# An attention and mixture-of-experts layer on one core: some early transfers issued by ScalarE's queue, and the steps in a new order

## The chip, the core and the metric

The kernel runs on one core of a Trainium2 chip. The core has five engines, each with its own instruction stream: TensorE (PE; PEld is its weight load), VectorE (DVE), ScalarE (ACT), GpSimd (POOL) and SyncE (SP). Here SP only issues DMA transfers. An engine runs its instructions strictly in order, so an instruction that waits on a semaphore holds up all that is behind it. The metric is the device time of one execution in microseconds.

## The reference

For each of 16 batches of 256 tokens with 128 features:

```
x = x + layernorm(attention(layernorm(x)))     # 16 heads of width 8, softmax(q k / sqrt(128)) v, then w_out
x = x + layernorm(moe(layernorm(x)))           # router to the top 2 of 8 experts (width 64), silu(gate) * up,
                                               # plus one shared expert of width 128
```

Inputs, outputs and weights are float32.

## The kernel before

A batch is one unit of work. Its steps are these, with the engine in brackets.

- `load_x` (SP), `stats1`, `aggr1` (DVE), `rstd1` (POOL) and `apply1` (ACT) are the first layer norm (LN1). `xT` (PE) and `xT_copy` (ACT) transpose the result. `qk` (PE) projects it to queries and keys in the PSUM bank `bank_a`.
- `part1` (ACT), `rest1` (DVE), `part2` (ACT), `part3` (POOL) split queries and keys into three bfloat16 parts, `parts`, whose products together give float32 accuracy.
- `spill` (SP) writes the parts to DRAM (`qk_dram`) in 6 transfers, 3 of queries and 3 of keys. `stack` (SP) reads them back in 4 transfers, 2 into `qs` (queries) and 2 into `ks` (keys), so that the parts of a head lie under each other on 48 partitions. Batch 0 does without DRAM: selection matrices (`lay0a`, `lay0b` on DVE, `lay1`, `lay2` on ACT) are written into `hidden`, and the matmuls `sel1`, `sel2`, `sel3`, `selq` place its parts; the semaphore `laid` counts them, and `kh_copy`, `kl_copy`, `ql_copy`, `qh_copy` move them to `ks` and `qs`.
- `s1_0` to `s1_7` (PE) compute scores of two heads each into one of two PSUM tiles `sc`. `max_0` to `max_7` (DVE, 1.2 us each) take the row maxima. `msplit` (POOL) splits the maxima into three parts, `maxT` (PE) transposes them, `max_copy` (ACT) moves them to `mT`, and `max_stack` (SP, 2 transfers `qs<-mT`) puts them below the queries as three more rows.
- `s2_0` to `s2_7` (PE) compute the scores again, transposed and with the maxima taken off, into the same two tiles `sc`. `exp_0` to `exp_7` (ACT, 1.0 us each) exponentiate. `pv_0` to `pv_3` (PE) multiply with the values.
- The sums go through DRAM once more (`pv_spill`, `den_load`, `pv_load`), are normalised, projected, normed (LN2), added. The expert part follows: LN3, `router`, five times `gu` (PE), `tanh` (ACT), `ha` and `hb` (DVE); expert weights through DRAM (`w_spill`, `w_load`); `hw` (POOL), `down` (PE), LN4, `store`.

Batches overlap. The order of every step on its engine is a table, `TIMES`: for each step a list of 16 ticks, one for each batch. Each engine walks over all ticks, and at each it emits the steps of its own that are due (`due(tick, name)`). The table sets only the order in each engine's stream; when a step really starts is decided by semaphores. `FILL` names places where PE multiplies `ident` by itself into `bank_d`, to stay busy.

All transfers are issued on SP's queue in the order of the table, and PE's scores go by strict turns: `s1` and `s2` of different batches alternate on the two `sc` tiles. The first instructions of `s1(b, 0)` wait for the four stacked transfers of batch b, and those of `s2(b, 0)` wait for the two of the maxima.

Of the kernel before, what the change touches and what calls it, by code (L numbers as in the profile page):

```python
# [12 lines left out]
P = 128  # L13
# [48 lines left out]
    "v_copy": [45, 88, 115, 121, 183, 263, 377, 444, 605, 705, 794, 928, 1033, 1142, 1271, 1395],  # L62
    "pickm": [47],
    "minusm": [50],
    "sel3": [51],
    "load_wd": [53],
    "ql_copy": [55],
    "kh_copy": [56],
    "selq": [59],
    "kl_copy": [60],  # L70
# [110 lines left out]
    "hwl0": [1892],  # L181
    "hwl1": [1894],
    "hwl2": [1895],
    "hwl3": [1896],
}


# [1050 lines left out]
```

## Time and profile before

| | us |
|---|---|
| median of 3 runs | 377.91 (376.65 to 379.62) |
| the profiled execution, device time | 378.36 |
| its span (first to last instruction) | 376.6 |
| busy, PE | 347.9 (92%) |
| busy, DVE | 312.3 (83%) |
| busy, ACT | 268.8 (71%) |
| busy, POOL | 200.2 (53%) |
| DMA engines, mean share on q1 | 48.6% |

Busy time of PE is modelled to the end of each pipelined matmul, so a busy PE is not a PE at its peak. The granted clock of PE is full for 98% of the span. In 40 slices of 9.4 us the page shows the busy tenths of each engine:

```profile
PE   6986898899999999999998999999999999998892
DVE  8498498978989999998997979989998996767661
ACT  5643668788887886877888887787669868964522
```

### The profile page before, as it was taken

What the parts mean: (1) busy time and instruction counts of PE and PEld (TensorE: products, weight loads), DVE (VectorE), ACT (ScalarE), POOL (GpSimd) and SP (SyncE); (2) the same over time, 40 slices, a digit from 0 to 9 for tenths busy, and PEclk for the clock granted to TensorE, in tenths of its full rate; (3) what the DMA queues carried; (4) which work ended last, traced back from release to release, by engine and by line L of the source; (5) the groups of instructions that cost most, each with busy time, mean ns of one, the idle gap of its engine ahead of it and who ended that gap; (6) DMA issues with size and microseconds to landing.
All of it is one profiled execution on the core that took longest, in us unless ns stands there. A gap on an engine that the chain in (4) does not pass through costs nothing.

```text
span 376.6 us, 9905 instructions
## 1 busy us (share of the span) xinstructions
PE 347.9 (92%) x3230; PEld 220.5 (59%) x3230; DVE 312.3 (83%) x788; ACT 268.8 (71%) x511; POOL 200.2 (53%) x518
## 2 busy tenths in 40 slices
PE   6986898899999999999998999999999999998892
PEld 6854444455465657574756565665665556666672
DVE  8498498978989999998997979989998996767661
ACT  5643668788887886877888887787669868964522
POOL 5623134305372584466666455765355648867644
PEclk9899899999999999999999999999999999999998
DMA  2457946716468466367265574734664241222210
GB/s 83 120 136 159 199 98 160 167 39 151 131 157 184 119 167 156 99 145 184 52 190 119 148 168 128 172 100 132 146 150 107 61 127 58 78 71 73 58 30 29
DMA packets 59921, 45.64 MB, mean 121 GB/s; under 512 B 8966, under 2 KB 56966, under 8 KB 59870
## 3 DMA queue, kind: packets, MB, share of 16 engines
q1 hardware_dynamic: 59870, 45.00, 48.6%
q8 instruction: 26, 0.43, 0.5%
q14 instruction: 25, 0.20, 0.2%
HBM read 26.69 MB, written 17.81 MB: 118 GB/s over the span
## 4 chain that ended last, share of the span: by engine, by line
PE 46%; POOL 15%; issue 13%; DVE 9%; ACT 6%; DMA 6%; SPq 4%; POOLq 1%; DVEq 0%; ACTq 0%
PE pvp L648 9%; PE bank_d L818 7%; PE sc L632 6%; PE bank_d L802 6%; PE sc L617 4%; DVE mx L997 4%; PE bank_d L803 4%; POOL hidden L1206 4%; POOL rstd L1139 3%; PE bank_a L701 3%; DMA qs<-mT 2%; ACT pr L846 2%; PE bank_d L775 1%; SPq L534 1%; DMA rwb<-rw_dram 1%
## 5 line engine op out<-in xcount | busy, mean ns | idle before, releaser
L997 DVE TENSOR_REDUCE mx<-sc 128x4 f32<-128x1024 f32 x128 | 154.0, 1218 | 20.1 <-PE sc L617 18.7
L846 ACT ACTIVATE pr<-sc 128x1024 f32<-128x1024 f32 x128 | 130.5, 1024 | 25.5 <-PE sc L632 24.2
L648 PE MATMUL pvp<-pr,va 128*32 128x256 f32 x1024 | 68.4, 385 | 0.0
L802 PE MATMUL bank_d<-x3T,wg_sb 128*128 128x256 f32 x160 | 54.8, 424 | 3.2 <-DVE hidden L1095 2.8
L632 PE MATMUL sc<-qs,ks 51*128 51x256 bf16 x512 | 50.2, 277 | 6.6 <-DMA qs<-mT 4.3
L617 PE MATMUL sc<-ks,qs 48*128 48x256 bf16 x512 | 49.4, 274 | 3.1 <-DMA ks<-qk_dram 1.0
L1206 POOL TENSOR_TENSOR hidden<-hidden,rwb 128x256 f32<-128x256 f32 x60 | 42.8, 728 | 16.4 <-DMA rwb<-rw_dram 16.4
L803 PE MATMUL bank_d<-x3T,wu_sb 128*128 128x256 f32 x160 | 47.7, 380 | 0.0
L1139 POOL TENSOR_TENSOR rstd<-vareps,mhalf 128x2 f32<-128x2 f32 x64 | 44.5, 695 | 0.0
L929 ACT ACTIVATE th<-bank_d 128x256 f32<-128x256 f32 x80 | 30.4, 382 | 16.7 <-PE bank_d L803 15.7
L648 PEld LDWEIGHTS pvp<-pr,va 128*32 128x32 f32 x1024 | 26.7, 109 | 25.4 <-issue 13.1
L818 PE MATMUL bank_d<-wd_sb,hidden 128*128 128x128 f32 x320 | 39.5, 279 | 1.9 <-POOL hidden L1206 1.7
L1089 DVE SCALAR_TENSOR_TENSOR ha<-th,bank_d 128x256 f32<-128x256 f32 x80 | 32.4, 407 | 9.4 <-ACT th L929 9.0
L1134 POOL TENSOR_TENSOR vareps<-mv,eps 128x2 f32<-128x2 f32 x64 | 12.4, 195 | 52.0 <-DVE mv L980 49.7
L818 PEld LDWEIGHTS bank_d<-wd_sb,hidden 128*128 128x128 f32 x320 | 37.1, 192 | 4.8 <-issue 2.3
L632 PEld LDWEIGHTS sc<-qs,ks 51*128 51x128 bf16 x512 | 16.4, 95 | 37.2 <-issue 15.2
L802 PEld LDWEIGHTS bank_d<-x3T,wg_sb 128*128 128x128 f32 x160 | 24.3, 189 | 19.1 <-issue 18.5
L617 PEld LDWEIGHTS sc<-ks,qs 48*128 48x128 bf16 x512 | 18.1, 95 | 26.7 <-issue 8.8
L1095 DVE SCALAR_TENSOR_TENSOR hidden<-ha,bank_d 128x256 f32<-128x256 f32 x80 | 32.6, 411 | 1.1 <-PE bank_d L818 0.2
L803 PEld LDWEIGHTS bank_d<-x3T,wu_sb 128*128 128x128 f32 x160 | 30.7, 192 | 4.3
L1150 POOL TENSOR_TENSOR parts<-rest,parts 128x512 bf16<-128x512 f32 x16 | 18.5, 1155 | 23.7 <-ACT parts L874 23.7
L1029 DVE RECIPROCAL rden<-den 128x256 f32<-128x256 f32 x14 | 24.4, 1741 | 0.2
(113 smaller groups left out, 488.6 us busy)
## 6 DMA issues: line engine op xcount, KB each, us to landing
rwb<-rw_dram SPq DMA_DIRECT2D x30, 256.0 KB, 4.3
qk_dram<-parts SPq DMA_DIRECT2D x30, 192.0 KB, 2.6
qs<-qk_dram SPq DMA_DIRECT2D x30, 192.0 KB, 4.6
ks<-qk_dram SPq DMA_DIRECT2D x30, 192.0 KB, 4.9
qk_dram<-parts SPq DMA_DIRECT2D x30, 128.0 KB, 2.6
pv_dram<-pv_sb SPq DMA_DIRECT2D x14, 256.0 KB, 2.3
x_sb<-in_L_attn_x_dram SPq DMA_DIRECT2D x16, 128.0 KB, 2.7
out_dram<-x SPq DMA_DIRECT2D x16, 128.0 KB, 1.9
```

Of the source, the lines that this page charges most:

```text
L617: mm = pe.matmul(sc[pair][:, u, c, :], q[rows, s, c * P:(c + 1) * P], k[rows, s, :], start=True, stop=True)
L632: mm = pe.matmul(sc[pair][:, u, c, :], k[rows, s, c * P:(c + 1) * P], q[rows, s, :], start=True, stop=True)
L648: mm = pe.matmul(pvp[32 * j:32 * j + 32, g, :], values[:, X * c + 4 * g + j, 32 * tt:32 * tt + 32], pr[:, k, c * N:(c + 1) * N], start=(tt ...
L802: pe.matmul(bank_d[bank][:, 0:N], wg_sb[:, ORDER[n], :], x3T[b % 2][:], start=True, stop=True)
L803: pe.matmul(bank_d[bank][:, N:2 * N], wu_sb[:, ORDER[n], :], x3T[b % 2][:], start=True, stop=True).then_inc(gu_done, 1)
L818: mm = pe.matmul(bank_d[0][:, c * P:(c + 1) * P], src, wd_sb[:, n, :], start=(n == 4), stop=(n == 3))
L846: nc.scalar.activation(pr[:, 2 * s:2 * s + 2, :].rearrange("p k n -> p (k n)"), sc[PAIR["s2", b, s]][:].rearrange("p u c n -> p (u c n)"), ...
L997: nc.vector.tensor_reduce(mx[b % 2][:, :, :, s].rearrange("p c u -> p u c"), sc[PAIR["s1", b, s]][:], AX.X, ALU.max).then_inc(max_done, 1)
L1089: nc.vector.scalar_tensor_tensor(out=ha[n][:], in0=th[n][:], scalar=1.0, in1=bank_d[BANK[n]][:, 0:N], op0=ALU.add, op1=ALU.mult).then_inc( ...
L1095: nc.vector.scalar_tensor_tensor(out=hb[b % 2][:, ORDER[n], :], in0=ha[n][:], scalar=0.5, in1=bank_d[BANK[n]][:, N:2 * N], op0=ALU.mult, o ...
L1139: nc.gpsimd.tensor_tensor(rstd[L][p][:], vareps[L][p][:], mhalf[:], ALU.pow).then_inc(rstd_done[L], 1)
L1206: nc.gpsimd.tensor_tensor(hw[b % 2][:, n, :].rearrange("p (t g r) -> p t g r", t=TT, g=4), hb[b % 2][:, n, :].rearrange("p (t g r) -> p t ...
```

## The change

The functions that issue one transfer of a spill, a stack or the maxima are taken out of SP's loop and given the issuing engine as an argument. For batch 1 the three key transfers of the spill (`spillA`) and the two key transfers of the stack (`stackA`) are issued by ACT, those of the queries by SP as before. For batch 0 the two transfers of the maxima are issued by ACT, right behind `max_copy`. For all other batches SP issues everything, as before. The table `TIMES` is a new one throughout. `FILL` loses most entries; a new table `FILL_SCORES` puts such matmuls in front of some `s1` and `s2`, behind the wait for the free tile and ahead of the wait for the transfers. Of LN1's neighbours at the start, `lay0a` now stands behind `aggr1` of batch 0, and `lay2` behind `xT_copy` of batch 0.

```diff
 FILL = {
-    "maxT": {0: 9},
+    "maxT": {0: 1},
     "qk": {0: 1},
-    "s1_3": {0: 2},
-    "s1_4": {0: 2, 1: 1},
-    "s1_5": {0: 2, 2: 1},
-    "s2_0": {0: 2},
-    "s2_4": {0: 2, 1: 1},
-    "s2_5": {0: 1},
     "sel1": {0: 2},
-    "xT": {0: 12, 3: 1},
+    "xT": {0: 17, 4: 1},
+}
+FILL_SCORES = {
+    ("s1", 0, 3): 1,
...
+    ("s1", 3, 7): 1,
...
+    ("s2", 1, 3): 2,
 }
...
+        def spill_k(engine, b, n):
+            first, slots = SLOTS_K[n]
+            dst = qk_dram[b % 2][1, first:first + slots].rearrange("a d u x n -> (d u x) a n")
+            engine.dma_start(dst, parts[b % 2][:, 1, 0:slots, :]).then_inc(qk_spilled[b % 2], DMA)
...
-                        sp.dma_start(dst, parts[b % 2][:, 1, 0:slots, :]).then_inc(qk_spilled[b % 2], DMA)
+                        spill_q(sp, b, n)
+                        if b > 1:
+                            spill_k(sp, b, n)
...
+                        stack_q(sp, b, u)
+                        if b > 1:
+                            stack_k(sp, b, u)
-                if (b := due(tick, "max_stack")) is not None:
+                if (b := due(tick, "max_stack")) is not None and b:
...
+                pair = PAIR["s1", b, s]
+                turn(sc_empty[pair])
+                fill_scores("s1", b, s, pair)
                 if b and s == 0:
                     pe.wait_ge(qk_stacked[b % 2], landed1(4, b))
...
             for tick in TICKS:
+                if due(tick, "spillA") is not None:
+                    act.wait_ge(part3_done, 2)
+                    for n in range(3):
+                        spill_k(act, 1, n)
+                if due(tick, "stackA") is not None:
+                    act.wait_ge(qk_spilled[1], landed1(6, 1))
+                    for u in range(2):
+                        stack_k(act, 1, u)
+                if due(tick, "max_stack") == 0:
+                    act.wait_ge(max_copied, 1)
+                    for u in range(2):
+                        stack_max(act, 0, u)
```

The first place that matters is SP's queue from the spill of batch 1 on. `qk_dram1<-parts1` is that spill, `qs1<-qk_dram1` and `ks<-qk_dram1` are the stack of batch 1, `qk_dram0<-parts0` is the spill of batch 2, `qs0<-mT0` are the maxima of batch 0. Before:

```order
L534 DMA qk_dram1<-parts1 128x3x256
L537 DMA qk_dram1<-parts1 128x3x256
...
L544 DMA qs1<-qk_dram1 48x2048
L546 DMA ks<-qk_dram1 48x2048
...
L534 DMA qk_dram0<-parts0 128x3x256
...
L478 DMA ks<-minus 3x4x2048 x2
L551 DMA qs0<-mT0 3x8x256 x2
L469 DMA x_sb6<-in_L0_attn_x_dram 128x2x128
L544 DMA qs2<-qk_dram0 48x2048
```

Now, on the same queue:

```order
L478 DMA qk_dram1<-parts1 128x3x256
L478 DMA qk_dram1<-parts1 128x2x256
L478 DMA qk_dram1<-parts1 128x256
L486 DMA qs1<-qk_dram1 48x2048 x2
L502 DMA x_sb5<-in_L0_attn_x_dram 128x2x128
L511 DMA ks<-minus 3x4x2048 x2
L478 DMA qk_dram0<-parts0 128x3x256
...
L483 DMA qk_dram1<-parts1 128x256
L486 DMA qs2<-qk_dram0 48x2048
```

The keys of batch 1 and the maxima of batch 0 have left the queue, the `minus` rows have moved ahead of the spill of batch 2, and the spill of batch 3 (the last `qk_dram1<-parts1`) has moved ahead of the stack of batch 2.

The second place is ACT's stream over the same stretch. `parts1<-rest1` is `part2` of batch 1, `va1` and `va2` are `v_copy` of batches 1 and 2, `mT0` is `max_copy` of batch 0, and `xn` is `apply1`. Before:

```order
L877 CAST ks<-sc0 112x1024
L874 CAST parts1<-rest1 128x2x256
L863 COPY xT0<-bank_a 128x256
L884 CAST qs0<-pvp 112x512
L885 CAST qs0<-bank_d0 112x512
L871 CAST parts0<-bank_a 128x2x256
L831 ACTIVATE xn1<-x_sb3,shift1_1,rstd1_1 128x128 x2
L874 CAST parts0<-rest0 128x2x256
L892 COPY va1<-bank_a 128x32x8
```

Now, from `part2` of batch 1 (`xn1<-x_sb3` stands just ahead of it):

```order
L919 CAST parts1<-rest1 128x2x256
L908 COPY xT0<-bank_a 128x256
L929 CAST qs0<-pvp 112x512
L930 CAST qs0<-bank_d0 112x512
L937 COPY va1<-bank_a 128x32x8
L483 DMA qk_dram1<-parts1 128x3x256
L483 DMA qk_dram1<-parts1 128x2x256
L483 DMA qk_dram1<-parts1 128x256
L916 CAST parts0<-bank_a 128x2x256
L490 DMA ks<-qk_dram1 48x2048 x2
L937 COPY va2<-bank_a 128x32x8
L919 CAST parts0<-rest0 128x2x256
```

Seven transfers now stand in ACT's stream (the two `qs0<-mT0` come right behind `max_copy`), and `apply1` of batch 3 has moved ahead of `part2` of batch 1.

The third place is DVE's start. `hidden<-ident_bf` are the copies of `lay0a` and `lay0b`, `st1_0<-x_sb0` is `stats1` of batch 0. Before:

```order
L953 MEMSET hidden 128x896
L988 COPY hidden<-ident_bf 128x8x24 x2
L988 COPY hidden<-ident_bf 128x8x2x8 x2
L988 COPY hidden<-ident_bf 128x8x8 x2
L991 MEMSET rw0 128x16
L991 MEMSET rw1 128x16
L973 BN_STATS st1_0<-x_sb0 128x6 x2
```

Now:

```order
L998 MEMSET hidden 128x896
L1033 COPY hidden<-ident_bf 128x8x2x8
L1033 COPY hidden<-ident_bf 128x8x8 x2
L1018 BN_STATS st1_0<-x_sb0 128x6 x2
L1025 BN_AGGR mv1_0<-st1_0 128x2 x2
L1033 COPY hidden<-ident_bf 128x8x24 x2
```

Three of the six copies and two memsets have moved from ahead of the first layer norm to behind it.

## Rows read from the trace of the kernel before

**Rows 1.** Busy us by stretch: PE, PEld, DVE, ACT, POOL; clock, DMA share, GB/s

```profile
20.00:47.00 27.00, 21.84 (x166) 12.83 (x166) 20.49 (x28) 12.56 (x24) 6.30 (x15) 0.94 0.76 172
...
80.00:320.00 240.00, 232.96 (x2311) 143.03 (x2304) 217.15 (x535) 191.12 (x354) 135.53 (x351) 1.00 0.53 132
```

**Rows 2.** The chain that ended last, 19 to 39 us: start, us, what

```profile
19.57 1.17 POOL parts L1150
...
23.32 2.40 DMA qk_dram<-parts
...
33.79 4.27 DMA qs<-mT
```

**Rows 3.** Timeline of SP's queue: start, us of issuing, line, transfer

```profile
20.75 0.37 SPq L534 DMA_DIRECT2D qk_dram<-parts  x1
...
27.04 0.42 SPq L546 DMA_DIRECT2D ks<-qk_dram  x1
...
32.69 2.97 SPq L551 DMA_DIRECT2D qs<-mT  x2
...
54.28 1.50 SPq L551 DMA_DIRECT2D qs<-mT  x2
```

**Rows 4.** Timeline of PE: start, us, instruction, idle before it and its releaser

```profile
7.59 0.44 PE L691 MATMUL bank_a<-ident,xn 128*128 128x128 f32 x2 [1.29 <-ACT xn L831]
...
8.58 1.81 PE L701 MATMUL bank_a<-xT,wqk_sb 128*128 128x256 f32 x4 [0.33 <-ACT xT L863]
...
16.30 1.03 PE L701 MATMUL bank_a<-xT,wqk_sb 128*128 128x256 f32 x4
...
28.64 2.27 PE L655 MATMUL bank_d<-ident 128*128 128x128 f32 x18
...
32.59 0.39 PE L617 MATMUL sc<-ks,qs 48*128 48x256 bf16 x4 [1.05 <-DMA ks<-qk_dram]
...
38.10 0.39 PE L632 MATMUL sc<-qs,ks 51*128 51x256 bf16 x4 [1.63 <-DMA qs<-mT]
...
57.29 0.39 PE L632 MATMUL sc<-qs,ks 51*128 51x256 bf16 x4 [0.97 <-DMA qs<-mT]
```

**Rows 5.** Timeline of DVE, columns as in rows 4

```profile
4.29 0.27 DVE L973 BATCH_NORM_STATS2 st<-x_sb 128x6 f32<-128x128 f32 x1
...
19.73 4.62 DVE L997 TENSOR_REDUCE mx<-sc 128x4 f32<-128x1024 f32 x4 [0.94 <-PE sc L617]
...
33.03 4.62 DVE L997 TENSOR_REDUCE mx<-sc 128x4 f32<-128x1024 f32 x4 [1.12 <-PE sc L617]
39.45 1.23 DVE L997 TENSOR_REDUCE mx<-sc 128x4 f32<-128x1024 f32 x1 [1.80 <-PE sc L617]
43.19 1.23 DVE L997 TENSOR_REDUCE mx<-sc 128x4 f32<-128x1024 f32 x1 [2.50 <-PE sc L617]
...
47.76 0.68 DVE L1020 TENSOR_TENSOR rest<-bank_a,parts 128x512 f32<-128x512 f32 x1
```

**Rows 6.** The copies of `lay0a` and `lay0b` by source line: ns min/median/max

```profile
L988 DVE COPY hidden<-ident_bf x6: 206/261/1498, 2.0 to 4.1; 128x192 bf16<-128x192 bf16 x2, 128x128 bf16<-128x128 bf16 x2, 128x64 bf16<-128x64 bf16 x2
```

**Rows 7.** Busy time in five shorter stretches, columns as in rows 1

```profile
8.80:12.20 3.40, 3.40 (x13) 2.89 (x13) 2.42 (x16) 1.77 (x4) 1.29 (x5) 0.50 0.40 94
21.00:25.70 4.70, 4.12 (x34) 2.69 (x34) 4.70 (x5) 1.98 (x4) 0.03 (x1) 1.00 0.70 197
26.00:32.60 6.60, 4.64 (x36) 3.33 (x36) 5.42 (x13) 1.51 (x4) 2.86 (x9) 1.00 0.94 185
39.50:42.90 3.40, 3.28 (x16) 1.74 (x16) 1.18 (x1) 1.94 (x5) 1.03 (x1) 0.51 1.06 160
73.70:77.10 3.40, 3.40 (x15) 1.95 (x14) 2.19 (x3) 1.61 (x2) 0.91 (x4) 0.50 0.50 152
```

**Rows 8.** Timeline of ACT: `apply1` of one batch, and `max_copy` of batch 0

```profile
21.53 0.88 ACT L831 ACTIVATE xn<-x_sb,shift,rstd 128x128 f32<-128x128 f32 x2
...
31.59 0.37 ACT L853 CAST mT<-bank_a 48x256 bf16<-48x256 f32 x1 [2.57 <-PE bank_a L670]
```

**Rows 9.** Waits of PE over the whole span: us in total, times, longest

```profile
PE sc L632 <- DMA qs<-mT: 4.3, 4, 1.6
```

More of the change, by code:

```diff
@@ L55 @@
-    "load_wgu": [33],
[6 rows of a table removed]
[L62 to L70, printed above, removed]
-    "s1_0": [64, 107, 165, 229, 283, 391, 493, 607, 700, 831, 932, 1069, 1179, 1290, 1386, 1515],
-    "qh_copy": [67],
-    "s1_1": [68, 114, 173, 238, 307, 407, 522, 621, 723, 852, 952, 1085, 1196, 1309, 1403, 1530],
@@ L179 @@
[L179 to L184 removed]
+    "load_x": [0, 12, 13, 15, 38, 95, 142, 185, 206, 208, 218, 280, 401, 473, 551, 822],
+    "lay0b": [14],
+    "stats1": [16, 23, 24, 50, 51, 139, 161, 221, 237, 247, 353, 378, 478, 664, 1013, 1106],
+    "lay1": [18],
+    "load_wout": [19],
+    "aggr1": [20, 27, 34, 52, 62, 160, 181, 231, 250, 347, 461, 526, 608, 683, 1119, 1169],
@@ new lines @@
+    "wv": [35],
+    "part1": [37, 61, 88, 110, 151, 209, 297, 432, 534, 666, 759, 876, 1008, 1118, 1230, 1354],
+    "rest1": [40, 66, 89, 112, 153, 217, 305, 441, 553, 670, 764, 882, 1010, 1124, 1235, 1359],
+    "sel1": [41],
+    "load_wgu": [42],
[5 rows of a table added]
+    "v_copy": [49, 80, 96, 129, 191, 262, 354, 459, 593, 711, 787, 931, 1055, 1177, 1265, 1432],
+    "sel3": [55],
+    "minusm": [57],
+    "ql_copy": [59],
+    "kh_copy": [60],
+    "selq": [63],
+    "pickm": [64],
+    "kl_copy": [65],
[3 rows of a table added]
+    "qh_copy": [76],
@@ new lines @@
+    "max_1": [78, 120, 178, 243, 314, 420, 533, 629, 725, 859, 967, 1084, 1203, 1318, 1430, 1550],
+    "s1_2": [79, 123, 180, 248, 324, 422, 535, 630, 734, 862, 980, 1096, 1210, 1326, 1440, 1553],
+    "spill": [None, 81, 108, 124, 188, 289, 341, 474, 587, 717, 803, 911, 1024, 1151, 1252, 1386],
+    "spillA": [82],
[5 rows of a table added]
+    "stack": [None, 91, 134, 146, 212, 327, 425, 524, 607, 752, 857, 989, 1086, 1193, 1288, 1419],
+    "stackA": [92],
+    "max_4": [93, 135, 195, 265, 343, 447, 559, 655, 775, 891, 1007, 1132, 1237, 1345, 1458, 1586],
@@ L599, in turn, with fill_scores @@
                     pe.wait_ge(*empty)
+            def fill_scores(kind, b, s, pair):
+                for _ in range(FILL_SCORES.get((kind, b, s), 0)):
+                    pe.matmul(sc[pair][:, 0, 0, 0:P], ident[:], ident[:], start=True, stop=True)
             def s1(b, s):
+                pair = PAIR["s1", b, s]
+                turn(sc_empty[pair])
+                fill_scores("s1", b, s, pair)
                 if b and s == 0:
@@ L621, in s2 @@
             def s2(b, s):
+                pair = PAIR["s2", b, s]
+                turn(sc_empty[pair])
+                fill_scores("s2", b, s, pair)
                 if s == 0:
```

141 lines of the change are left out of this document (71 added, 70 removed), and 156 rows, old and new, of the table TIMES.

## The prediction

> **What bounds the kernel now.** I read the busy time by stretch first [rows 1]. From 80 to 320 us PE is busy for 232.96 of 240 us and DVE for 217.15, so 97% and 90%. There two engines share the bound, and each loses time only by waiting for the other. The start is different: from 20 to 47 us PE is busy for 21.84 and DVE for 20.49 of 27. What is to be had is there, since the new table leaves the tail with the same steps in nearly the same sequence.
>
> The chain of waits says what the start waits for [rows 2]. It passes from POOL's `part3` of batch 1 into SP, stays in SP's queue and its transfers from 20.75 to 38.06 us, and ends with the 4.27 us of the maxima transfer. SP's timeline [rows 3] shows why. The spill of batch 1 is issued from 20.75 on, the last of its six at 23.32. The four of the stack follow, the last at 27.04. Behind them stand the spill of batch 2 and the `minus` rows, so the maxima, which ACT had copied by 31.96 [rows 8], are issued only at 32.69, and these two issues take 2.97 us where the next pair takes 1.50.
>
> PE and DVE show the price [rows 4, 5]. PE gets batch 1's scores going at 32.59, released by the keys of the stack, and batch 0's `s2_0` at 38.10, released by the maxima. DVE waits 1.12 us ahead of the first maximum of batch 1, 1.80 ahead of the fifth, 2.50 ahead of the sixth. The last ends at 47.8.
>
> PE's granted clock is the other loss. It is at half, 1.2 GHz, for 3.4 us from 8.8, from 39.5 and from 73.7 us [rows 7]. The first time comes after PE sat idle for 1.29 us ahead of `xT`, and `qk` then takes 1.81 us where the next takes 1.03 [rows 4]; the second comes after the waits for the maxima.
>
> **The change part by part.** Times are against the profiled span of 376.6 us.
>
> *Start of LN1.* `stats1` of batch 0 begins at 4.29, behind six copies. Now three copies stand ahead of it. The first of the six took 1498 ns, the shortest 206, the median 261 [rows 6]. The long one comes first in time, beside POOL's memset of `hidden`, and in the new order the first is still beside it. So the three take about 1.50 + 0.21 + 0.21 = 1.9 us from 1.96, and `stats1` starts at about 3.9: 0.4 us gained. The bound if the long copy were gone would be 1.7.
> The Trainium skill, "SBUF — State Buffer", on the shared port pair, says that a GpSimd instruction and a VectorE instruction in a two-port mode lock each other out for the whole instruction. By that rule it is the first copy, whichever it is, that waits, and the gain is the 0.4 us; the one row of 1498 ns agrees.
>
> *Fills ahead of `xT`.* Seventeen instead of twelve. Five more are ten records, at 2.27 us for 18 [rows 4] about 1.2 us, which covers the 1.29 us in which PE sat idle. If the clock then stays up, `qk` takes 1.03 instead of 1.81, and the first selection matmuls, which also lie ahead of 12.2 us, save some 0.5 more (an estimate: one us of them at half clock). I take 0.9 of these 1.3, because the clock may fall all the same. If it does, the fills cost nothing but the stretch at half clock stays. With the 0.4 above, `laid` and the copies behind it are 1.3 us earlier.
>
> *`apply1` of batch 3 ahead of `part2` of batch 1.* It adds 0.88 us of ACT to the chain, as the two `apply1` activations take [rows 8]. `part3` of batch 1, which ended at 20.73, now ends at 20.3: 0.4 us gained, not 1.3.
>
> *Spill of batch 1 on two queues.* Six issues at about 0.5 us become three beside three. No transfer was issued by ACT in this trace; the nearest rows are SP's, from 0.33 us for a quiet one to 1.5 (half of 2.97) for one behind a full queue [rows 3], and I take SP's 0.5, since ACT's own queue is empty. Issuing then ends at 21.8. The DMA engines bound the rest: from 21.0 to 25.7 they were busy for 0.70 of 4.7 us [rows 7], that is 3.3 us, so the last lands no sooner than about 20.3 + 0.6 + 3.3 = 24.2, with 0.6 as my estimate for the first packets to set out. Before it landed at 25.72: 1.5 us gained, of which 0.4 were there already.
> The Trainium skill, "DMA: Bandwidth & Descriptors", section "Issuing engines are not separate DMA queues", speaks against expecting more: all queues run on the same 16 DMA engines, and issuing from several saves only the sequencer's time. By it this step is worth at most 1.5 us of saved issuing; the row of 3.3 us busy limits it to 1.1, so here it is the row that is tighter.
>
> *Stack of batch 1.* Two issues beside two: the last is issued at 24.7 instead of 27.04. It landed at 32.5, 5.5 us later, in a stretch in which the DMA engines were busy for 0.94 of 6.6 us [rows 7], because SP put the spill of batch 2 right behind it. Now `x` of batch 5, `minus` and the wait for `part3` stand between, so I take 4.7 us for it. It lands at 29.4, and the first maximum of batch 1 starts at 29.9 instead of 33.03: 3.1 us gained. If the landing stays 5.5 us, it is 2.3.
>
> *Maxima of batch 0 on ACT.* `maxT` follows `s1_1` of batch 1, so the copy can start about 1.2 us after 29.5 and, with its 0.37 [rows 8], ends at 31.1. Two issues take 1.5 to 2.1 us and the landing 1.5 to 2.3 behind them (the pair at 54.28 ended at 55.78 and released PE at 57.29 [rows 3, 4]). `s2_0` starts at 34.1 to 35.5, I take 34.8: 3.3 us earlier than 38.10.
>
> *DVE after that.* With four maxima from 29.9 it waits about 1.1 us for the fifth instead of 1.80. Ahead of the sixth PE has `s2_1`, `qk`, `s2_2`, `s1_5`. At full clock this wait is 1.4 instead of 2.50; at half clock it stays. So batch 1's last maximum is earlier by 3.1 + 0.7 + 1.1 = 4.9 at full clock, by 3.8 at half. I take the middle, 4.4.
>
> *What ACT's transfers cost.* ACT is busy for 12.56 of these 27 us [rows 1]. But ACT stands still at the wait for `qk_spilled`, until 24.2. Behind it `v_copy` of batch 2 holds `bank_a`, which `xT` of batch 3 needs, and `s1_7` of batch 0 stands behind that on PE. By my times `v_copy` ends at 25.5. DVE's first maximum moves from 19.73 to 18.4 [rows 5], and seven at 1.16 with one `rest1` at 0.6 bring it to 27.1, when it wants `s1_7`. So it costs nothing up to 1 us of delay, and one for one beyond.
>
> *The other fills.* 39 before, 38 now. One in front of an `s1` takes 0.2 us behind the wait for the tile while DVE works 1.2 us on the other: hidden. They are meant for the clock; the stretch from 73.7 may go, which is worth about 1 us. I take half: 0.5.
>
> *The rest of the table.* From 80 us on the counts of instructions are the same. PE waits four times for the maxima, 4.3 us in all [rows 9], two of them in the start above. I take zero for the new sequence, with 3 us to either side as the bound: that is about what one more or fewer wait in each fourth batch makes.
>
> The sum is 4.4 + 0.5 = 4.9 us. Span 376.6 - 4.9 = 371.7. The profiled execution took 378.36, so 1.8 lie around the span, and it was 0.45 above the median of the runs. That gives 371.7 + 1.8 - 0.45 = 373.0; I predict **373.2 us**. All figures are of one execution, and about 1% is what a measurement of this kernel can tell from no change, here 3.8 us.
>
> **The rivals.**
> *A: as forecast, 0.55.* The gain at 47 us is kept, because both bounding engines are near their limit from there and simply start earlier. 370 to 374.1.
> *B: gained and given back, 0.20.* SP now has the spill of batch 3 ahead of the stack of batch 2, and in some batches (2 and 6) about 3 us of PE's work stand between the maxima transfer and `s2_0`, where there were 4 and 9. Two waits of 1.0 to 1.6 us, as [rows 4, 9] show, leave 4.9 - 2.6 = 2.3: about 375.8.
> *C: little gained at the start, 0.12.* The transfers share the DMA engines, which were busy for 0.94 from 26 to 32.6 us, and the clock falls in all three places. Then the start gives 0.4 + 1.1 at the spill and some of the maxima, 1.5 to 2 us: about 376.2. The chain [rows 2], which is in SP's issuing and not only in landing, speaks against it.
> *D: slower, 0.13.* The mechanism is the maxima reaching PE late in the middle. A wait of 1.6 us there was followed by 3.4 us at half clock, in which PE loses up to 1.7 more: 3.3 a time. The gain of 4.9 is used up after one and a half of them, and from three on (9.9) the kernel is slower by more than 1%: about 383. For it speaks that PE goes by strict turns; against it that the clock was full from 80 to 320 us in spite of two such waits.
>
> **How the numbers follow.** Faster by over 1% (below 374.1) is A: 0.55. Within 1% are B and C: 0.32. Slower is D: 0.13. The range is 370.0 to 378.0: below lies the case that the middle also gains 3, above it the bulk of D.
>
> **What would show it.** In the profile after: `stats1` at 3.9; `qk` of batch 0 near 1.0 us; the stack's release of `s1_0` of batch 1 near 29.4; `s2_0` of batch 0 near 34.8 and DVE's last maximum of batch 1 ending at 43.4; the half clocks from 8.8 and 39.5 gone. The sum is wrong if ACT's issues take over 1 us each, if PE is held at `xT` of batch 3, or if the stretch from 47 to 320 us is not as long as before.

## The result, and the profile after

The changed kernel is slower: 385.71 us median of 4 runs (382.79 to 389.03), where the kernel before had 377.28 on the same chip. The ratio is 1.0207, with an interval of 1.0143 to 1.0271; it leaves out the run of 389.03, which counts as a slow one. So the kernel is slower, clear of noise; whether by more than 2% is open. The forecast was 373.2, so the sign was wrong too.

| | before | after |
|---|---|---|
| profiled execution, us | 378.36 | 389.03 |
| its span, us | 376.6 | 387.2 |
| granted clock over the span | 0.983 | 0.965 |
| TensorE at half clock, us: mean over the runs | 11.3 (105 runs) | 22.9 (4 runs) |

The last line is worked out from each run's span and mean granted clock, as 2 x (1 - clock) x span. By this a mean clock of 0.983 is 12.8 us at half clock, 3.4% of the span; the 98% given for the kernel before is the mean clock, not the share of the time at full clock. The profiled execution of after is the longest of its four, so its later stretches at half clock are more than the median run has. Its waits up to 41 us are not peculiar to it: e3, the same program up to there, shows them within 0.2 us.

Up to 28 us the times are near the forecast ones or earlier. PE's and DVE's timelines of the changed kernel, columns as in [rows 4]:

```profile
1.51 5.59 PE L688 MATMUL bank_d<-ident 128*128 128x128 f32 x34 [1.51 <-POOL ident L1167]
...
8.07 1.10 PE L734 MATMUL bank_a<-xT,wqk_sb 128*128 128x256 f32 x4 [0.33 <-ACT xT L908]
...
27.42 0.61 PE L630 MATMUL sc<-ident 128*128 128x128 f32 x4
31.17 0.61 PE L649 MATMUL sc<-ks,qs 48*128 48x256 bf16 x8 [3.14 <-DMA ks<-qk_dram]
...
36.09 1.20 PE L744 MATMUL bank_a<-wv_sb,xT 128*128 128x128 f32 x4 [1.36 <-ACT xT L908]
38.86 0.61 PE L665 MATMUL sc<-qs,ks 51*128 51x256 bf16 x4 [1.58 <-issue]
```

```profile
1.95 1.62 DVE L1033 COPY hidden<-ident_bf 128x128 bf16<-128x128 bf16 x3
3.49 0.48 DVE L1018 BATCH_NORM_STATS2 st<-x_sb 128x6 f32<-128x128 f32 x2
...
17.76 4.62 DVE L1042 TENSOR_REDUCE mx<-sc 128x4 f32<-128x1024 f32 x4 [0.73 <-PE sc L649]
...
31.60 2.36 DVE L1042 TENSOR_REDUCE mx<-sc 128x4 f32<-128x1024 f32 x2 [2.67 <-PE sc L649]
...
40.78 1.23 DVE L1042 TENSOR_REDUCE mx<-sc 128x4 f32<-128x1024 f32 x1 [4.08 <-PE sc L649]
```

DVE's first maximum starts at 17.76 instead of 19.73 [rows 5], 2.0 us earlier. But 1.2 of these lie in the one execution of the kernel before that was profiled. e4, e5 and e10, described below, run the old program up to there; in their traces the clock stays full at 8.8 us. PE and DVE of e10:

```profile
7.59 0.44 PE L691 MATMUL bank_a<-ident,xn 128*128 128x128 f32 x2 [1.06 <-ACT xn L831]
...
8.58 1.10 PE L701 MATMUL bank_a<-xT,wqk_sb 128*128 128x256 f32 x4 [0.33 <-ACT xT L863]
```

```profile
18.48 4.62 DVE L997 TENSOR_REDUCE mx<-sc 128x4 f32<-128x1024 f32 x4 [0.94 <-PE sc L617]
```

Against these three (18.48 to 18.50) the changed kernel gains 0.7 us, and at batch 1's scores nothing: they come at 31.17, where the profiled before has 32.59 but e4 31.33 and e10 30.69. `s2_0` of batch 0 starts at 38.86, behind the 38.10 of before [rows 4]. SP's queue and ACT with its queue show the transfers (for a queue: start, us of issuing):

```profile
19.76 1.78 SPq L478 DMA_DIRECT2D qk_dram<-parts  x3
23.94 0.81 SPq L486 DMA_DIRECT2D qs<-qk_dram  x2
...
27.03 1.59 SPq L478 DMA_DIRECT2D qk_dram<-parts  x1
28.67 1.79 SPq L483 DMA_DIRECT2D qk_dram<-parts  x1
```

```profile
19.77 1.86 ACTq L483 DMA_DIRECT2D qk_dram<-parts  x3
...
23.94 0.84 ACTq L490 DMA_DIRECT2D ks<-qk_dram  x2
...
32.58 0.36 ACT L898 CAST mT<-bank_a 48x256 bf16<-48x256 f32 x1 [3.00 <-PE bank_a L703]
32.98 2.49 ACTq L494 DMA_DIRECT2D qs<-mT  x2
35.57 0.37 ACT L908 COPY xT<-bank_a 128x256 f32<-128x256 f32 x1 [2.62 <-issue]
```

The stack is issued by 24.78, 2.7 us earlier than the 27.46 of [rows 3], yet lands at 31.12: 6.3 us behind. The maxima keep ACT issuing for 2.49 us, and `xT_copy` of batch 4, behind them in ACT's program, starts 2.62 us late. The chain of waits has the same two pieces (start, us, what):

```profile
24.34 6.78 DMA ks<-qk_dram
...
32.98 1.35 ACTq L494
34.33 0.37 issue
34.70 0.76 ACTq L494
...
35.57 0.38 ACT xT L908
```

And the clock, in busy time by stretch, columns as in [rows 1]; the second group is the stretches at half clock:

```profile
20.00:47.00 27.00, 19.72 (x126) 10.95 (x126) 16.33 (x18) 8.73 (x16) 3.21 (x6) 0.75 0.87 189
...
80.00:320.00 240.00, 230.49 (x2266) 142.84 (x2264) 215.53 (x520) 187.66 (x346) 130.54 (x335) 0.99 0.53 135
...
26.00:32.60 6.60, 3.46 (x27) 2.28 (x26) 3.61 (x4) 2.21 (x6) 3.06 (x6) 0.96 1.03 199
```

```profile
32.10:45.70 13.60, 10.66 (x61) 5.37 (x60) 7.06 (x8) 4.18 (x6) 0.00 (x0) 0.50 0.94 201
49.10:55.90 6.80, 6.37 (x50) 2.49 (x52) 2.55 (x6) 2.93 (x4) 3.04 (x9) 0.50 0.00 1
```

Between 20 and 47 us PE is busy for 2.1 us less than before and DVE for 4.2 less. PE sat idle for 3.14 us ahead of the stack, and from 32.1 us it was at half clock for 13.6 us on end. Before, 18 fill products, 2.27 us, stood in front of that wait; the change has 4 there (27.42), and 2 of `maxT`'s behind it. (A fill of the tables shows as two products in a trace: the 9 of `maxT` are these 18.)

### The profile page after: what moved, and what is told of

Read it like the earlier page. It is cut to its first block, busy times and chain, and to the rows that moved or that the text cites. A ratio compares the mean times of both kernels' runs of the same rounds, so it can differ in the third digit from the quotient of the medians.

```text
span 387.2 us, 9900 instructions
## 1 busy us (share of the span) xinstructions
PE 350.5 (91%) x3228; PEld 222.7 (58%) x3228; DVE 311.5 (80%) x788; ACT 267.8 (69%) x511; POOL 201.0 (52%) x518
## 4 chain that ended last, share of the span: by engine, by line
PE 40%; issue 20%; POOL 14%; DVE 9%; DMA 7%; ACT 6%; SPq 2%; ACTq 1%; POOLq 1%; DVEq 0%
PE pvp L681 7%; PE bank_d L851 6%; PE sc L665 6%; PE bank_d L835 5%; POOL hidden L1251 4%; DVE mx L1042 4%; PE sc L649 4%; PE bank_d L836 3%; POOL rstd L1184 3%; DMA qs<-mT 2%; PE bank_a L734 2%; ACT pr L891 2%; DMA ks<-qk_dram 2%; PE bank_d L688 2%; DVE ha L1134 1%
## 5 line engine op out<-in xcount | busy, mean ns | idle before, releaser
L681 PE MATMUL pvp<-pr,va 128*32 128x256 f32 x1024 | 71.0, 396 | 0.0
L649 PE MATMUL sc<-ks,qs 48*128 48x256 bf16 x512 | 50.4, 278 | 5.3 <-DMA ks<-qk_dram 3.1
L1251 POOL TENSOR_TENSOR hidden<-hidden,rwb 128x256 f32<-128x256 f32 x60 | 42.2, 729 | 21.8 <-DMA rwb<-rw_dram 19.8
L851 PE MATMUL bank_d<-wd_sb,hidden 128*128 128x128 f32 x320 | 41.0, 285 | 3.6 <-POOL hidden L1251 3.6
L974 ACT ACTIVATE th<-bank_d 128x256 f32<-128x256 f32 x80 | 30.6, 383 | 17.2 <-PE bank_d L836 15.8
L851 PEld LDWEIGHTS bank_d<-wd_sb,hidden 128*128 128x128 f32 x320 | 38.7, 199 | 6.6 <-issue 6.1
L835 PEld LDWEIGHTS bank_d<-x3T,wg_sb 128*128 128x128 f32 x160 | 24.2, 188 | 19.3 <-issue 19.0
L649 PEld LDWEIGHTS sc<-ks,qs 48*128 48x128 bf16 x512 | 19.0, 96 | 26.1 <-DVE mx L1042 7.9
```

The source lines that it names most:

```text
L649: mm = pe.matmul(sc[pair][:, u, c, :], q[rows, s, c * P:(c + 1) * P], k[rows, s, :], start=True, stop=True)
L681: mm = pe.matmul(pvp[32 * j:32 * j + 32, g, :], values[:, X * c + 4 * g + j, 32 * tt:32 * tt + 32], pr[:, k, c * N:(c + 1) * N], start=(tt ...
L835: pe.matmul(bank_d[bank][:, 0:N], wg_sb[:, ORDER[n], :], x3T[b % 2][:], start=True, stop=True)
L851: mm = pe.matmul(bank_d[0][:, c * P:(c + 1) * P], src, wd_sb[:, n, :], start=(n == 4), stop=(n == 3))
L1251: nc.gpsimd.tensor_tensor(hw[b % 2][:, n, :].rearrange("p (t g r) -> p t g r", t=TT, g=4), hb[b % 2][:, n, :].rearrange("p (t g r) -> p t ...
```

## The experiments

Ratios are to the kernel before on the same chip; a median stands beside the others only roughly, since those of the kernel before went from 376.4 to 378.2 between chips and hours. So versions are compared by their ratios, 0.1% being 0.38 us. One chip each had e1 to e4, e5 to e8, e9 to e12, and e13 to e16.

| run | median us | ratio, interval | half clock, mean us |
|---|---|---|---|
| changed kernel | 385.71 | 1.0207, 1.0143 to 1.0271 | 22.9 |
| e1_all_sp | 383.61 | 1.0136, 1.0059 to 1.0212 | 19.7 |
| e2_fills | 379.43 | 1.0037, 0.9997 to 1.0077 | 7.3 |
| e7_fills_sp | 376.21 | 1.0000, 0.9957 to 1.0042 | 5.0 |
| e13_keys_act | 376.31 | 0.9960, 0.9919 to 1.0001 | 6.7 |
| e14_maxima_act | 382.91 | 1.0141, 1.0082 to 1.0201 | 13.1 |
| e17_keys_act_13_5 | 377.61 | 0.9999, 0.9956 to 1.0041 | 7.2 |
| e5_act_only | 382.66 | 1.0177, 1.0113 to 1.0241 | 21.1 |
| e3_head_new | 395.18 | none | 37.3 |
| e4_head_old | 382.57 | 1.0131, 1.0019 to 1.0243 | 17.2 |
| e12_old_head | 377.91 | 1.0002, 0.9961 to 1.0043 | 8.7 |
| e6_sp_behind | 379.77 | 1.0093, 1.0052 to 1.0134 | 10.5 |
| e9_stack_alone | 383.76 | 1.0145, 1.0026 to 1.0263 | 17.6 |
| e10_maxT_fills | 377.71 | 1.0011, 0.9970 to 1.0051 | 15.3 |
| e8_start | 376.28 | 0.9959, 0.9914 to 1.0004 | 10.2 |
| e16_start_only | 378.24 | 0.9981, 0.9936 to 1.0026 | 12.0 |
| e11_start_fills | 377.38 | 1.0025, 0.9991 to 1.0058 | 5.7 |
| e15_start_six | 376.64 | 0.9975, 0.9945 to 1.0005 | 3.8 |

**All transfers back on SP, and longer fills.** e1 puts the three groups of transfers back on SP in the new order; e2 keeps them on ACT and lengthens two fills; e7 does both.

```diff
     # e1_all_sp, e7_fills_sp (the three blocks on ACT go)
-                        if b > 1:
-                            spill_k(sp, b, n)
+                        spill_k(sp, b, n)
-                if (b := due(tick, "max_stack")) is not None and b:
+                if (b := due(tick, "max_stack")) is not None:
     # e2_fills, e7_fills_sp
-    ("s1", 1, 0): 2,
+    ("s1", 1, 0): 16,
+    ("s2", 0, 0): 8,
```

> The changed kernel with its new table, but all transfers issued by SP again. If the issuing by ACT is what costs (ACT stood at its own two maxima issues for 2.5 us, and the copy behind them was 2.6 us late), this comes back by 2 to 4 us, to about 381. If the new order at the start and PE's half clock in it are what costs, it stays within 2 us of the changed kernel (383 to 388) or is worse, since SP's queue holds the maxima behind two spills again.

> The changed kernel with more ident matmuls ahead of two waits: 16 instead of 2 ahead of the first scores of batch 1, 8 ahead of the first second-pass scores of batch 0. If the loss is PE's half clock from 32 to 46 and from 49 to 56 us after a wait of 3.1 us without work, the clock stays full there and the time falls by 5 to 8 us, to about 378. If the late transfers alone cost, the clock row changes and the time stays within 1.5 us of 385.

> The changed kernel's order with the longer fills (16 and 8), and every transfer issued by SP as before. It undoes ScalarE's issuing at a clock that the fills hold up. Theory 1 (ScalarE's issuing of the maxima costs, the rest of it gains nothing): the first second-stage product of batch 0 starts 1.5 to 2.5 us earlier than the 40.3 with ScalarE's issuing, and the time is 377 to 379, 1 to 2 us under 379.4. Theory 2 (ScalarE's issuing is not what costs; the order is): within 0.7 us of 379.4, or slower by the later stack.

By the ratios, fills alone take 1.7% off, 6.4 us, and 1.4%, 5.1 us, with all transfers on SP (e1 to e7). Moving the transfers to SP takes off 0.7% with the short fills; the intervals overlap, so e1 alone decides nothing. With the long fills it is 0.9%, 3.5 us, between e6 (which is e2 over again, see below) and e7 on the same chip; between e2 and e7, on two chips, it is 0.4%. So there are two causes, the fills' being the larger. In e2 PE does not stand idle ahead of the stack, and the clock holds there; the maxima still hold ACT, and ahead of `s2_0` the clock falls:

```profile
27.79 3.73 PE L631 MATMUL sc<-ident 128*128 128x128 f32 x32
31.46 0.61 PE L650 MATMUL sc<-ks,qs 48*128 48x256 bf16 x8
...
37.01 3.32 PE L631 MATMUL sc<-ident 128*128 128x128 f32 x16
40.26 0.39 PE L666 MATMUL sc<-qs,ks 51*128 51x256 bf16 x4
```

The upper 32 products take 3.73 us at full clock, the lower 16 take 3.32, most of it at half. In e7 those 16 took 2.05 and `s2_0` stood at 37.27, 3.0 us earlier, more than either theory had.

**Which of ACT's transfers.** Both with e2's fills: e13 leaves the keys on ACT and puts the maxima back on SP, e14 the other way round.

```diff
     # e13_keys_act
-                if (b := due(tick, "max_stack")) is not None and b:
+                if (b := due(tick, "max_stack")) is not None:
-                if due(tick, "max_stack") == 0:
-                    act.wait_ge(max_copied, 1)
-                    for u in range(2):
-                        stack_max(act, 0, u)
```

> The changed order with the longer fills (16 and 8); ScalarE's queue issues the keys of batch 1's spill and stack, SP the two maxima transfers of batch 0. With all on SP this was 376.2 us, with keys and maxima on ScalarE 379.4. Theory 1 (the maxima transfers are what costs on ScalarE: they stand there for 2.5 us at a time when its queue holds x's copies and the exponentials): 376 to 377.3. Theory 2 (the keys on ScalarE cost as well, by the 0.4 us that the stack lands later): 377.5 to 379.5.

> The fourth corner beside the three: longer fills, ScalarE issues the maxima transfers alone, SP all keys. Theory 1: 378.5 to 380, ScalarE stands about 2.5 us at the two transfers, and the first second-stage product of batch 0 starts at 39.5 to 40.5. Theory 2 (the maxima are late only where the DMA engines are also loaded by ScalarE's keys): 376 to 378, with the two issues under 1.5 us.

Keys on ACT: 376.31 (theory 1). Maxima on ACT: 382.91, slower than both theories had. The ratios are 1.8% apart on one chip, 6.8 us. ACT's own timeline of e14 first, then SP's queue, ACT and PE of e13:

```profile
33.22 2.10 ACTq L495 DMA_DIRECT2D qs<-mT  x2
35.43 0.37 ACT L899 COPY xT<-bank_a 128x256 f32<-128x256 f32 x1 [2.23 <-issue]
```

```profile
32.84 1.50 SPq L495 DMA_DIRECT2D qs<-mT  x2
...
33.39 0.37 ACT L905 COPY xT<-bank_a 128x256 f32<-128x256 f32 x1 [0.59 <-PE bank_a L725]
...
37.11 0.39 PE L666 MATMUL sc<-qs,ks 51*128 51x256 bf16 x4
```

In e14 `s2_0` starts at 39.67. The path is: two issues hold ACT for 2.1 us, `xT_copy` of batch 4 waits behind them, PE has `v` of batch 3 ahead of `s2_0` in its program and stands until that copy frees the buffer, and its fills, now at half clock, follow. How the 6.8 us divide is not shown. 6.4 us more at half clock would be 2.4 at the 0.38 found below; `s2_0` is 2.6 later, part of it by that clock. Nor is it shown why the maxima alone on ACT measure slower than keys and maxima together: e14's `s2_0` is no later than e2's 40.26, and its ratio is 1.0141 against 1.0037 (e2) and 1.0093 (e6).

**ACT's issuing in the old order.** e5 has before's table and fills, and the three groups on ACT.

> The kernel before with its own order and its own fills; of the change only one part is left: ScalarE's queue issues the key transfers of batch 1's spill and stack and batch 0's two maxima transfers. Theory 1 (the transfers are limited by what the 16 DMA engines carry, not by which queue issues them, and ScalarE stands while it issues): the stack of batch 1 lands where it did, within 0.7 us of 32.5, ScalarE stands 2 to 2.5 us at the maxima transfers (2.49 in the changed kernel), the first second-stage product of batch 0 starts 1 to 2.5 us behind 38.1, and the time is 378.5 to 381.5 us against 377. Theory 2 (the issuing on two queues is what the change gains by, and the order lost it): the stack lands at 29.5 to 31, the second-stage product starts at 36 to 37, and the time is 375 to 376.5.

It is 1.8% slower by itself, on theory 1's side and beyond its bounds: the two maxima issues take 2.70 us, and `s2_0` starts at 40.91. Here the trace has a wait behind the keys as well; what it alone costs was not run. ACT stands at its wait for `qk_spilled` in a place where the old order has `v_copy` behind it, PE then waits for that copy, and again behind the maxima:

```profile
26.98 0.41 PE L717 MATMUL bank_a<-ident,xn 128*128 128x128 f32 x2 [2.23 <-ACT va L930]
...
37.10 0.68 PE L737 MATMUL bank_a<-wv_sb,xT 128*128 128x128 f32 x4 [2.20 <-ACT va L930]
40.91 0.61 PE L658 MATMUL sc<-qs,ks 51*128 51x256 bf16 x4 [1.72 <-DVE mx L1035]
```

**What limits the stack's landing.** e6 moved three SP steps in the table; since SP has nothing else between them, its queue stayed as it was, and the run is e2 over again: 379.77 beside 379.43, with ratios of 1.0093 and 1.0037. So far apart can one kernel lie on two chips. e9 is e7 with a real wait.

```diff
     # e9_stack_alone; fills 10 instead of 16
                 if (b := due(tick, "load_x")) is not None:
+                    if b == 5:
+                        sp.wait_ge(qk_stacked[1], landed1(4, 1))
```

> The changed kernel with the longer fills of the run before (16 and 8 products in place of 2 and 0), and three steps of SP moved: the load of x's tile 5, the minus ones' load and batch 2's spill stand behind the first scores of batch 1 and no longer right behind batch 1's stack. Theory 1 (the stack lands late, 6.4 us behind its last issue, because its packets share the DMA engines with what SP puts right behind it): the stack lands 1.5 to 2.5 us earlier, at 29 to 30 instead of 31.2, and the first max of batch 1 with it; what this gives at the end is open, since batch 2's spill is later by 3 to 5 us, 377 to 380. Theory 2 (the landing is the time that the stack's own descriptors take, whatever is behind them): it lands at 30.9 to 31.5 again, and the kernel is slower than the 379.4 of the kernel it is built from, 380 to 383, by batch 2's later stack.

> The changed order with all transfers on SP and the longer fills (10 products before batch 1's first scores, 8 before batch 0's second stage), and one wait more: SP waits until batch 1's stack has landed before it issues x's tile 5, the minus ones and batch 2's spill. (A run before this one was meant to move these behind by their steps alone, but nothing of it changed SP's own order.) Theory 1 (the stack's landing 5.6 to 6.4 us behind its last issue is partly the traffic put behind it): the stack lands at 29.3 to 30.3 instead of 31.2, and since batch 2's spill then comes 2 to 3 us later and its stack with it, the time is 376 to 378.5 against the 376.2 without the wait. Theory 2 (the 768 KB of the stack alone take this long): it lands at 31.0 to 31.6, and the time is 377.5 to 380.

PE's timeline of e9, then of e1, in which SP goes on issuing behind the stack:

```profile
30.34 0.61 PE L650 MATMUL sc<-ks,qs 48*128 48x256 bf16 x8 [0.42 <-DMA ks<-qk_dram]
```

```profile
30.75 0.61 PE L647 MATMUL sc<-ks,qs 48*128 48x256 bf16 x8 [2.75 <-DMA ks<-qk_dram]
```

With nothing behind it the stack, issued by 25.83, lands 4.5 us later; with `x`, `minus` and the next spill behind it, issued by about 25.7, 5.0 us later. These are single executions. e10, which has the whole spill of batch 2 right behind the stack, lands it 4.5 us behind its last issue too, and the profiled before 5.1. So the traffic behind is not shown to cost anything, and most of the time is the 768 KB themselves. These are the traces in which PE waited for the stack, from the first of its four issues to the landing of the last:

| trace | keys issued by | first issue | landed | us |
|---|---|---|---|---|
| before, e4, e16 | SP | 25.74, 24.49, 24.54 | 32.54, 31.28, 31.04 | 6.8, 6.8, 6.5 |
| e1, e10, e9 | SP | 23.98, 24.45, 24.11 | 30.70, 30.63, 30.29 | 6.7, 6.2, 6.2 |
| after, e3, e17 | ACT | 23.94, 24.19, 24.55 | 31.12, 31.29, 31.97 | 7.2, 7.1, 7.4 |

From two queues the last issue ends 0.9 us earlier (24.78 in after, 25.7 in e1), and the stack takes 0.3 to 1.2 us longer. What the second queue saved in issuing it did not save in landing. In e9 the landing is theory 1's and the time neither's: by the ratios it is 5.5 us slower than e7. Batch 2's spill starts at 32.48 instead of 28.2, the maxima behind it are issued only from 38.00, and PE stands for 4.64 us ahead of `s2_0`.

**The halves of the table.** e3 is the changed kernel up to batch 0's `pv_3` with before's order behind; e4 before's order up to `pv_copy` of batch 0 and the new one behind; e12 is e4 with the change's start and with fills of 4 and 8.

> The new order and ACT's transfers up to pv_3 of batch 0 (about 60 us), and from there the old order. If the whole loss arises in the first 60 us, this is as slow as the changed kernel, 383 to 388. If the new order of the middle costs too (its lag grew by 2 to 4 us between 68 and 387 us), this is 2 to 4 us faster than the changed kernel, about 381.

> The reverse: the old order and SP's transfers up to pv_copy of batch 0, and the new order behind it. If the loss arises in the first 60 us, this is within 1.5 us of the kernel before, 377. If the new order of the middle costs by itself, it is 380 to 381.

> The change's start, before's order from there to the end of batch 0's attention, the change's order from there on; all transfers on SP, fills as in the run that had the start alone (376.3). It tells whether the order behind 47 us is worth anything. Theory 1 (the rest of the table is neutral; the changed kernel loses ahead of it): 375.5 to 377, as the run with the start alone. Theory 2 (the rest of the table loses 1.5 us or more by itself): 378 to 380. Theory 3 (it gains, and the head hides it): under 375.

e3 tells nothing of the change, and no ratio is given for it: at the seam PE waited 6.52 us for a DVE maximum at 62 us, a stall that neither kernel has. e12 is level with before, theory 1: where the fills are long, the order behind batch 0 neither gains nor loses by more than 0.4%. e4 is 1.3% slower, outside both its cases and by an interval that starts at 0.2%; its mean at half clock is 17.2 us against 8.7 in e12. Its trace has 10.2 us at half from 33.1 on, which is inside the part with before's order, where the profiled before has 3.4. So e4 does not tell whether the new order behind, without fills, loses by itself.

**The start, and the fills of the kernel before.** e16 is before with the change's start alone; e8 adds fills of 4 and 8 ahead of the two waits; e11 six more small ones; e15 takes 6 instead of 9 ahead of `maxT`, and 5 and 6 ahead of the two waits. e10 is before with one number changed:

```diff
     # e10_maxT_fills
-    "maxT": {0: 9},
+    "maxT": {0: 1},
```

> The kernel before with the change's start alone (the layout copy behind LayerNorm's first aggregate, 17 fills instead of 12 ahead of x's first transpose), no other fill and no other order. The prediction priced these at 1.3 us of its 4.9, and half clock at 8.8 us would be gone. Theory 1 (the gain arrives at the end): 374.5 to 376, and batch 0's last max 1 to 2 us earlier. Theory 2 (it is swallowed by the wait for batch 1's stack, or by half clock later): 376.5 to 378.

> The kernel before with two things of the change and no more: the new order up to the first projection (the layout copy behind LayerNorm's first aggregate, the 17 fills ahead of x's first transpose), and fills while TensorE waits for batch 1's stack and batch 0's maxima (4 and 8 products). All transfers on SP, before's order behind. Theory 1 (what the change gains ahead of 20 us is real, and the loss comes behind it from the clock and the transfers): no half clock at 8.8 and at 39.5 us, batch 0's last max 0.4 to 1.5 us earlier, and the time is 373.5 to 376. Theory 2 (the start is worth nothing, the stack's landing swallows it, and half clock costs little): 376.5 to 378.

> The kernel before with the change's start (the layout copy behind LayerNorm's first aggregate, 17 fills ahead of x's first transpose) and fills ahead of waiting scores: 4 and 8 products at batch 1's first scores and batch 0's second stage as in the run before, and now 4, 2, 1, 1, 1, 1 more at six places of batches 1 to 3, where TensorE waits in that run's trace. Theory 1 (what is left over 372 is half clock in the first 80 us): the stretches at half clock at 56.0 and 73.1 go, and the time is 373 to 375.5. Theory 2 (the fills only stand in the way of work, or the clock falls elsewhere): 376 to 378.

> A candidate: the kernel before with the change's start, 6 fills ahead of the maxima's transpose instead of 9 (that transpose waited 2.3 us behind them, and the kernel before with 1 of the 9 had its batch 1 end 3.2 us earlier, though at half clock for 6.8 us), and 5, 6, 4, 2, 1, 1, 1, 1 fills at waiting scores of batches 0 to 3. Theory 1 (both gains add where the clock holds): 373 to 375.5. Theory 2 (the time at the end hangs on where the clock falls later, which fills up to 70 us don't set): 376 to 378.

> The kernel before with one number changed: 1 fill instead of 9 (2 products instead of 18, 2.27 us) ahead of the transpose of batch 0's maxima, as the change has it. Theory 1 (these fills carry TensorE's clock over the wait for batch 1's stack, and half of the change's loss is their going): half clock from about 32 us for 7 to 14 us, and a time of 379 to 382 us against 376.5. Theory 2 (the clock falls elsewhere for other causes; the fills are worth their place, no more): 375.5 to 377.5.

None differs from before by more than its interval. Batch 0's last maximum, which ends at 29.98 in the profiled before, ends at 28.25 to 29.40 in e16, e8, e11 and e15. But in e4 and e10, which lack the new start, it ends at 28.76 and 28.74, so what the start is worth lies between 0.7 us lost and 0.5 gained. A reason for the loss is in the traces: the 34 products of the 17 fills take 5.5 to 7.0 us, and in e11 and e16 `xT` starts behind them only at 8.30 and 7.70, where the old start has it at 7.58 to 7.60 in each trace. In e11:

```profile
1.51 6.95 PE L688 MATMUL bank_d<-ident 128*128 128x128 f32 x34 [1.51 <-POOL ident L1155]
8.30 0.38 PE L724 MATMUL bank_a<-ident,xn 128*128 128x128 f32 x2
```

In e10 PE stood for 2.15 us ahead of `maxT` and was at half clock from 29.8 us for 6.8 (with all its fills the old program has 3.4 us in this stage in one trace and 10.2 in another, e4). The mean at half was 15.3 us, against 10.7 for the kernel before on the same chip. By the price below that is 1.7 us; the interval reaches to 1.9. So in the old order these fills are worth little, where in the new one the wait was 3.14 us, the late maxima followed it, and the stretch was 13.6.

**The best of it.** e17 is e13 with 13 and 5 fills.

> The run with the keys on ScalarE, the maxima on SP and long fills (ratio 0.996), with 13 and 5 fills instead of 16 and 8: in that run's trace the fills ended at 31.3 and 37.1 us, right against the products behind them, so that they may hold back what has landed. Theory 1 (the fills hid 0.3 to 0.7 us at each of the two places, and the clock holds): batch 0's second stage starts at 36.3 to 36.8 instead of 37.1, ratio 0.990 to 0.996. Theory 2 (nothing had landed before, or the clock falls again once the fills are shorter): 0.996 to 1.003.

Level with before, theory 2. The stack released PE at 32.01 and the maxima at 37.60, both behind the fills' end. In this execution 16 fills would have ended ahead of 32.01 and hidden nothing, and 8 at about 38.0 (35.99, where they start, and the 2.05 us of e7's), 0.4 us too late. No version beat the kernel before by more than the measurement tells.

**What half clock costs.** Over 105 runs of the kernel before, all one program, the time rises by 0.38 us for each us at half clock (a line through the runs; correlation 0.77; 0.33 to 0.42 chip by chip). Such a line can't tell what the clock costs from what the late data cost that made it fall. But it fits where only fills were added: the changed kernel to e2 has 15.6 us less at half and is 6.4 faster (5.9 by the line), and e1 to e7 14.7 less and 5.1 faster (5.6). By it the 11.6 us more at half clock in the changed kernel are 4.4 of its 7.8 us (2.07%). What the other 3.4 are is not separately shown. The nearest is e6 against e7, 3.5 us for ACT's transfers, but with 5.5 us more at half clock in it, 2.1 by the line: no run has the maxima on ACT at a clock that held.

## Why the prediction was wrong

*Start of LN1: right, and undersized.* Forecast 3.9, measured 3.49, with the three copies at 1.62 us in all. The longest of the copies is now 1466 ns, beside the same memset of `hidden` on POOL, though another form stands in front; that agrees with the rule on the shared port pair on the Trainium skill's page "SBUF — State Buffer", "Who interferes with whom", by which of a VectorE instruction in a two-port mode and a GpSimd instruction the second to start is blocked until the first has ended. No run was made to test it.

*Fills ahead of `xT`: met by luck.* `qk` took 1.10 us and there is no half clock at 8.8. But with the twelve old fills e4, e5 and e10 have the same 1.10 and the same full clock behind idle times of 1.06 to 1.73 us. The forecast took for a property of the kernel what one of four traces of the old start shows, so its 0.9 us are not the fills' doing. Nor are the fills free, as the forecast had them: in e11 and e16 they delay `xT`.

*`apply1` of batch 3 ahead: not shown.* `part3` of batch 1 ended at 19.74 (forecast 20.3), but in e4 and e10, in the old order, at 19.5.

*Spill of batch 1: right in its times.* Issued by 21.6 (forecast 21.8), landed by 23.9 (forecast 24.2). The second queue is not why: e1, with all six on SP, landed at 23.96. The 0.6 us for the first packets came from no row; in the trace of the kernel before, the DMA engines stay idle from the first issue at 20.75 to about 21.65, 0.9 us.

*Stack of batch 1: the first step that failed.* The last issue began at 24.34 (forecast 24.7), but "I take 4.7 us for it" was 6.8, counted like the forecast from that issue's start (6.3 from its end). The reasoning that `x`, `minus` and a wait for `part3` would leave the engines free was wrong: DMA's share from 26 to 32.6 us is 1.03 where it was 0.94 [rows 7]. Nor was batch 2's spill what made it 5.5 before: e10 has that spill behind and took 4.9. The gain is 1.4 us at PE against the profiled before, not 3.1, and none against e4, e10 and e16. The rule "Issuing engines are not separate DMA queues" on the Trainium skill's page "DMA: Bandwidth & Descriptors", by which a second engine saves only the sequencer's time, is borne out, and more strongly than I used it: e7, with the keys on one queue, is level with e13, and the landings from two queues took longer.

*Maxima of batch 0 on ACT: failed by its sign.* Forecast `s2_0` at 34.8; measured 38.86. The copy `mT` was done at 32.94 instead of 31.1, by the late stack; the two issues took 2.49 us, above my bound of 2.1; and `s2_0` started 3.4 us behind them, where the landing was to take up to 2.3 (the profile names no releaser; that it was the landing is by elimination). SP did the two in 1.5 us (e13).

*What ACT's transfers cost: the step behind the wrong sign.* I checked only the wait for the spill, and that part holds: `v_copy` of batch 2 ended at 25.25 (forecast 25.5). I did not list what stands behind the maxima's issues on ACT, which is `xT_copy` of batch 4, and behind that `v` and `s2_0` on PE. For the keys the step holds in the new order (e13 against e7); in the old one e5's trace has a wait of 2.23 us behind them.

*The other fills: failed.* "39 before, 38 now" counted them and did not ask where they stand. I priced them at a gain of 0.5; in the new order they are the largest loss. What the number hid is that the wait for the stack had 18 products in front of it and got 4. Long fills there (32 products) and ahead of `s2_0` (16) recover 5.1 to 6.4 us; that is more than the kernel before had, and in the old order taking 16 of the 18 away cost nothing that can be told (e10).

*DVE after that* falls with its inputs: batch 1's last maximum came 2.1 us later than before, not 4.4 earlier.

*The rest of the table: right at zero where fills hold the clock* (e12); without them it is open (e4). But the head's gain is not at the end even where the clock holds: in e7 batch 1's last maximum is 2.1 us earlier than before, batch 2's 0.2, and the median is level. From there PE waits for ACT's exponentials, 0.73 and 0.90 us, and 0.95 at 58.57; the old order has 0.20 at 39.62 and 0.43 at 58.80:

```profile
43.22 0.71 PE L629 MATMUL sc<-ident 128*128 128x128 f32 x4 [0.73 <-ACT pr L878]
...
45.38 0.49 PE L629 MATMUL sc<-ident 128*128 128x128 f32 x2 [0.90 <-ACT pr L878]
```

The first of these lies ahead of batch 1's last maximum, so it is in the 2.1 already. That is rival B's mechanism in small, at another wait. That it is the whole of what was given back was not tried.

Rival D had the right side and half of the mechanism: late maxima followed by half clock. It put them in the middle and one by one; they came at batch 0, with a stretch of 13.6 us instead of 3.4. Rival C, that the transfers share busy DMA engines and little is gained at the start, was right about the transfers.

## What to carry to other kernels

Before a transfer goes to a compute engine's queue, list what stands behind it in that engine's program and who waits for that: two small transfers on ScalarE cost 3.5 us here beside the keys and 6.8 alone, where compared on one chip, while the keys' issues, with nothing urgent behind them, cost none. A table of fills is priced by which wait each fill stands in front of, never by its total. Where the DMA engines were already busy for 0.94 of a transfer's time, issuing from two queues did not bring its landing forward. And before a loss at one place is put into a forecast, look for it in a second trace of the same program: the half clock at 8.8 us was in one of four.

## What was not expected of the hardware

Issuing the two 12 KB transfers of the maxima took ACT's queue 2.10 to 2.70 us (after, e2, e3, e5, e6, e14), and SP's 1.50 or 1.51 in the new order (e1, e7, e9, e13, e17). But in the old order it took SP 2.96 to 3.02, the 2.97 of [rows 3] among them. There the two issues stand right behind the load of `minus`, and in all nineteen traces the two issues right behind that load are slow, whatever they are: 2.7 to 3.7 us for the two, where quiet ones take 0.33 to 0.5 each. (Single slow ones, up to 2.15 us, come elsewhere too.) The stack in flight is not the cause: the profiled before issues six transfers while it flies, at 0.42 to 0.69 each. And in e9 the stack had landed at 30.29 when these were issued:

```profile
30.81 1.61 SPq L512 DMA_DIRECT2D ks<-minus  x2
32.48 1.06 SPq L479 DMA_DIRECT2D qk_dram<-parts  x1
33.59 1.87 SPq L484 DMA_DIRECT2D qk_dram<-parts  x1
```

In the new order the two slow issues fall on batch 2's spill instead of the maxima. What it is about `minus` was not tried, nor was moving `minus` alone.

An idle stretch of 3.1 us was followed by 13.6 us at half clock, with PE busy for 10.66 of them, while the old start, with PE idle for 1.06 to 1.73 us ahead of `xT`, fell to half clock in one trace of four. Half clock is cheaper than it looks: about 0.38 us per us.
